# Half of the projections of queries, keys and values moved by one score step in the TensorE order

## The chip, the cores and the metric

The kernel runs on one core of a Trainium2 chip. The metric is the device time of one launch in microseconds (us). Engines are named as in the profile: PE is TensorE (its weight loads are PEld), DVE is VectorE, ACT is ScalarE, POOL is GpSimd, SP is SyncE, which issues the DMAs here.

## The reference

One layer of a macaron block on x of 32 samples, 512 positions, 256 features, in float32: a half-weighted routed feed-forward, attention, and the same feed-forward again, each on the layernorm of its input and added to it.

```python
x = x + 0.5 * ffn(layernorm(x))    # per sample: top 2 of 8 experts, chosen by its first row
x = x + attn(layernorm(x))         # 16 heads of 16, rotary positions, causal softmax
x = x + 0.5 * ffn(layernorm(x))
# attn: q, k, v = split(x @ Wqkv.T); q, k = q * cos + rotate_half(q) * sin, ...
#       out = softmax(mask(q @ k.T / 4)) @ v; return out @ Wo.T
```

## The kernel before, in words

The three parts follow each other; at the two seams they overlap a little. All that is changed lies in the attention.

**Slots.** Attention goes by groups of four heads, four groups to a sample. One turn of the loop is a slot; slot g (0 to 3) of sample s belongs to the group G = 4 s + g. No planner is in play: every engine has its own written order within a slot, and semaphores tie them together. `main` writes the slots of 30 samples out, `lead_in` puts six slots in front, between feed-forward steps. In one slot, three groups are under way:

- group G: the row maxima of its scores. PE computes scores with queries on the partitions (`max_scores`, 11 steps, L1158 to L1167), DVE takes the maximum of each (`maxima`, L996 and L1006).
- group G-2: its scores again, keys on the partitions, with the negative maximum as an added row (`scores`, 10 steps, L1185). ACT takes the exponential of each (`exps`, L1073), POOL masks the diagonal blocks in four pieces (`mask`, L912), and PE multiplies with the values (`probs_v`, L1202). The first of four such products stands in this slot behind step 9, the other three in the next slot.
- group G-3: those three products behind step 3; ACT copies the sum (L1104), PE turns it (`turn_output`, four transposes, L1255) behind step 6, DVE normalises (`normalise_output`, L1016 and L1020). `probs_v` of G-2 writes the same bank and so waits for L1020.

A step is one index n of the loop in PE's `slot`; the text counts from 1, so step 6 is n = 5. `scores` of step n waits for the exponential two steps before (two banks), `max_scores` for the maximum three steps before (three banks).

**Work of other samples in the slots.** The sample that comes next is prepared in the same slots. Slots 0 and 1: its queries and keys, 128 features at a time (`project_qk`, L1219, t = 0 to 3). Each of them is six matmuls 128x512 in two halves of three, one behind an early step and one behind a later step of the slot. Slot 2: its values (`project_v`, L1233), six matmuls 128x256 for each of four blocks of 128 positions. Slot 3: transposes of the sample after that (L1247), and the output projection of the sample before (L1271, L1280). All of these use two banks, `x_ps`.

**Rotary positions.** When both halves of a projection are done (`qk_done`), DVE multiplies by cos (L974) and swaps neighbours (L975) in `begin_rope`, behind maximum 3 or 7 of the slot. POOL (`rope`) multiplies by sin (L920) and adds (L924), between its masks: t = 0 and 2 in the middle of slots 0 and 1, t = 1 and 3 at their end, behind the last mask. ACT rounds to float16 (L1079, `rope_high`), DVE computes what is left over (L981, `rope_low`, behind maximum 1 and 4 of slots 1 and 2). SP writes the result to memory and reads it back into stacks for the next sample's slots.

**Layernorm of the sample after next** stands in slot 2 behind maximum 2: DVE's statistics (L107 to L119), POOL's normalisation (L942, L948).

**Values.** ACT copies the finished values from the bank in `v_copy` (L1122), behind exponentials 5 and 8 of slot 2.

Of the kernel before, what the change touches and what calls it, by code (L numbers as in the profile page):

```python
# [58 lines left out]
def wait(eng, sem, value):  # L59

    if isinstance(value, int) and value <= 0:
        return
    eng.wait_ge(sem, value)
# [690 lines left out]
def attention(nc, ctx, tab, mem, src, dst, cos, sin, first):  # L754
# [49 lines left out]
    def group(G):  # L804
        return not isinstance(G, int) or 0 <= G < B * 4

    def sample(s):
        return not isinstance(s.b, int) or 0 <= s.b < B
# [321 lines left out]
    def tensor(pe):  # L1130
        def part(t, p):
            return t.hi if p == "hi" else t.lo

        def turn_maxima(s, g):

            G = 4 * s.b + g
            pe.wait_ge(max_done, 11 * G)
            nc.tensor.transpose(mx_ps[TURN_BANK][0:NT * GH, 0:P], mx[(g - 1) % 2][:].rearrange("p a i -> p (a i)"),
                                tab.ident[:]).then_inc(mt_done, 1)

        def max_scores(s, g, n):

            G = 4 * s.b + g

            if n == 4:
                wait(pe, mt_copied, G)
            else:
                wait(pe, max_done, 11 * G + (-2, -1, 1, 2, None, 3, 4, 5, 6, 7, 8)[n])
            if n == 0:
                pe.wait_ge(q_stacked, 96 * (s.b + 1))  # L1150
                pe.wait_ge(k_stacked, 96 * (s.b + 1))
            bank = mx_ps[MX_BANK[n]]
            i, heads = (3, [n]) if n < 4 else (2, [n - 4]) if n < 8 else (1, [2 * n - 16, 2 * n - 15]) if n < 10 else (0, range(4))
            w, nh = (i + 1) * P, len(heads)
            half, j = half_of(g)
            rows, const = slice(HP * half, HP * half + TERMS_ROWS), slice(HP * half, HP * half + HP)
            if n < 4:
                nc.tensor.matmul(bank[:, 0:w], q_stack[s.par][rows, j + n % 4, i * P:(i + 1) * P],  # L1158
                                 k_stack[s.par][rows, j + n % 4, 0:w], start=True, stop=True).then_inc(mx_done, 1)
                return  # L1160
            for at, a in enumerate(heads):
                nc.tensor.matmul(bank[:, at * w:at * w + w], q_stack[s.par][rows, j + a, i * P:(i + 1) * P],  # L1162
                                 k_stack[s.par][rows, j + a, 0:w], start=(at == 0), stop=False)

            last = bank[:, 0:nh * w].rearrange("p (a n) -> p a n", a=nh)[:, :, i * P:w]
            over = tab.mask[const, :].rearrange("p (a n) -> p a n", a=1)
            nc.tensor.matmul(last, tab.turn[const, :], over.broadcast_to([HP, nh, P]), start=False, stop=True).then_inc(mx_done, 1)  # L1167

        def scores(s, g, c):

            G = 4 * s.b + g - 2
            ss, sg = of_group(s, g, 2)
            bank = st_ps[c % 2]

            wait(pe, exp_done, 10 * G + c - 1)
            if c == 0:
                pe.wait_ge(rows_set[g % 2], 16 * (2 * s.b + (g - 2) // 2 + 1))
            a = c % 4 if c < 8 else 2 * (c - 8)
            half, j = half_of(sg)
            rows = slice(HP * half, HP * half + TERMS_ROWS + 1)  # L1180

            work = [(a, 0, 0, 0)] if c < 4 else [(a, 1, P, 0), (a, 3, 3 * P, 3 * P)] if c < 8 else \
                [(a, 2, 2 * P, 0), (a + 1, 2, 2 * P, 2 * P)]
            for ha, kt, q0, col in work:
                ins = nc.tensor.matmul(bank[:, col:col + T - q0], k_stack[ss.par][rows, j + ha, kt * P:(kt + 1) * P],  # L1185
                                       q_stack[ss.par][rows, j + ha, q0:T], start=True, stop=True)
            ins.then_inc(st_done, 1)

        def probs_v(s, g, lag, nth, kt):

            G = 4 * s.b + g - lag
            ss, sg = of_group(s, g, lag)
            if kt == 0:

                wait(pe, on_done, G)
                pe.wait_ge(v_copied, 2 * (ss.b + 1))
            pe.wait_ge(exp_done, 10 * G + (4, 8, 10, 8)[kt])
            pe.wait_ge(masked, 4 * G + nth + 1)
            for a in range(GH):
                p = (probs[:, a, :], probs[:, 4 + a, 0:3 * P], probs[:, 8 + a // 2, (a % 2) * 2 * P:(a % 2) * 2 * P + 2 * P],  # L1200
                     probs[:, 4 + a, 3 * P:])[kt]
                ins = nc.tensor.matmul(pv_ps[32 * a:32 * a + 32, kt * P:T], v[ss.par][:, kt, head_of(sg, a), :], p,  # L1202
                                       start=(kt == 0), stop=(nth == 3), tile_position=(0, 32 * a))
            ins.then_inc(pv_done, 1)

        def project_qk(n, t, half):

            idx = 4 * n.b + t
            if t == 0 and not half:
                pe.wait_ge(xT_lo, NC * (n.b + 1))  # L1210
            if n.b == 0 and not half:
                pe.wait_ge(first.xT_lo, NC * (FIRST_LEAD + 4 + t // 2))
            if t < 2 and not half:

                wait(pe, res_done, 2 * (n.b - 2) - 1 + t)
            if t >= 2 and not half:
                pe.wait_ge(rope_in, idx - 1)
            for i, (wp, xp) in enumerate(TERMS):
                ins = nc.tensor.matmul(x_ps[t % 2][:], part(tab.qkv, wp)[:, int(half), t * P:(t + 1) * P],  # L1219
                                       part(xT, xp)[:, int(half), :], start=(i == 0 and not half), stop=(i == 2 and half))  # L1220
            if half:
                ins.then_inc(qk_done, 1)

        def project_v(n, t):

            if t % 2 == 0:
                pe.wait_ge(rope_in, 4 * (n.b + 1) - 1 + t // 2)
                if n.b == 0:
                    pe.wait_ge(first.xT_lo, NC * B)
            i = 0  # L1230
            for c in range(NC):
                for xp, wp in TERMS:
                    ins = nc.tensor.matmul(x_ps[t // 2][:, (t % 2) * D:(t % 2) * D + D], part(xT, xp)[:, c, t * P:(t + 1) * P],  # L1233
                                           part(tab.qkv, wp)[:, c, 2 * D:3 * D], start=(i == 0), stop=(i == 3 * NC - 1))
                    i += 1
            if t % 2:
                ins.then_inc(v_done, 1)
# [48 lines left out]
        def slot(s, g, between=None):  # L1286
            G = 4 * s.b + g
            cur, run = group(G), group(G - 2)
            if G == 0:
                pe.wait_ge(first.gelu_done, 8 * B)  # L1290
            if G == 2:
                pe.wait_ge(stacks_set, 32)
                pe.wait_ge(first.out_done, 2 * B)
            if G == 6:
                pe.wait_ge(stacks_set, 64)
            before = group(G - 3)
            for n in range(11):
                if between:
                    between(n)
                if run and n < 10:  # L1300
                    scores(s, g, n)
                if cur:
                    max_scores(s, g, n)
                if n == 2 and before:
                    probs_v(s, g, 3, 1, 1)
                if n == 1 and group(G - 1):
                    turn_maxima(s, g)
                if n == 2 and before:
                    probs_v(s, g, 3, 2, 3)
                    probs_v(s, g, 3, 3, 2)  # L1310
                if n == 5 and before:
                    turn_output(s, g)
                if g < 2 and sample(s + 1) and n in (0, 1, 4, 5):
                    project_qk(s + 1, 2 * g + (n > 3), half=(n in (1, 5)))
                if g == 2 and sample(s + 1) and n in (0, 1, 4, 5):
                    project_v(s + 1, (0, 1, 4, 5).index(n))
                if g == 3 and sample(s + 2) and n == 0:
                    transposes(s + 2)
                if run and n == 8:
                    probs_v(s, g, 2, 0, 0)  # L1320
                if g == 3 and sample(s + -1) and n == 4:
                    transpose_o(s + -1, s)
                if g == 3 and sample(s + -1) and n >= 9:
                    project_o(s + -1, 2 * (n - 9))
                    project_o(s + -1, 2 * (n - 9) + 1)
# [285 lines left out]
```

## Time and profile before

| | |
|---|---|
| time, median of 3 runs | 2292.76 us (2287.46 to 2299.47) |
| the profiled execution | 2291.23 us, span 2289.5 us |
| PE busy | 2109.5 us, 92% |
| DVE busy | 1931.8 us, 84% |
| ACT busy | 1354.4 us, 59% |
| POOL busy | 1306.6 us, 57% |
| chain that ended last | PE 45%, DVE 33%, SP queue 7%, issue 6%, DMA 5%, ACT 4% |

Busy times are summed over the span of one profiled execution. Matmuls are pipelined and their ends are modelled, so a busy PE need not be one at its peak. The chain is followed back from the last instruction: at each step to what released it, or to the instruction before it on its engine. The stretch from 560 to 1806 us is attention alone; what lies before and behind is feed-forward and the two seams.

### The profile page before, as it was taken

Reading aid. Unit: us, or ns where it says so; the run is one execution under the profiler, and the core shown is the slowest. Engines: PE = TensorE matmul, PEld = TensorE weight load, DVE = VectorE, ACT = ScalarE, POOL = GpSimd, SP = SyncE. Lnnn points to the kernel's source line nnn. Section 1 sums busy time; section 2 is a strip of 40 time slices with the busy share of each in tenths; the row PEclk is TensorE's granted clock in tenths of the full one; section 3 lists DMA queues with packets and bytes.
Section 4 is the critical chain, followed back from the end, with each engine's and each line's share of the span. In section 5 each row is a group of like instructions: output and inputs, shape, how many; then the busy total and the mean of one; then the engine's idle time right before and its main releaser. Section 6 shows DMA issues by size and latency. Waiting matters only on the chain.

```text
span 2289.5 us, 52899 instructions
## 1 busy us (share of the span) xinstructions
PE 2109.5 (92%) x17682; PEld 1141.4 (50%) x17682; DVE 1931.8 (84%) x4485; ACT 1354.4 (59%) x2568; POOL 1306.6 (57%) x1462
## 2 busy tenths in 40 slices
PE   4999999889999999999999999999999888999999
PEld 2666666434444444444444444444444434666666
DVE  6777788788999899999989998999999865777776
ACT  3455444266667666666666676666666655445553
POOL 6666667454555455456545554554555425666664
PEclk9999999899999999999999999999999999999999
DMA  6656666444445444444444454444445423666665
GB/s 208 192 192 207 201 203 200 116 89 89 98 95 101 94 94 98 89 94 93 99 89 100 95 101 94 96 92 96 93 94 98 99 70 118 197 202 194 204 207 167
DMA packets 280391, 295.29 MB, mean 129 GB/s; under 512 B 45784, under 2 KB 263224, under 8 KB 280120
## 3 DMA queue, kind: packets, MB, share of 16 engines
q1 hardware_dynamic: 280120, 291.90, 50.3%
q8 instruction: 143, 2.34, 0.5%
q14 instruction: 128, 1.05, 0.2%
HBM read 140.08 MB, written 83.89 MB: 98 GB/s over the span
## 4 chain that ended last, share of the span: by engine, by line
PE 45%; DVE 33%; SPq 7%; issue 6%; DMA 5%; ACT 4%; DVEq 0%; ACTq 0%
PE bank L710 8%; DVE bank L996 7%; DVE at_mx L1006 7%; PE bank L728 7%; PE bank L1185 6%; PE bank L1202 6%; PE bank L1219 4%; PE bank L1280 4%; ACT probs L1073 3%; DVE turned L975 3%; DVE v_qk L981 3%; DVE turned L974 2%; DVE at_stats L107 2%; PE bank L1255 2%; PE bank L1167 2%
## 5 line engine op out<-in xcount | busy, mean ns | idle before, releaser
L1073 ACT ACTIVATE probs<-bank 128x512 f32<-128x512 f32 x1280 | 747.0, 603 | 456.9 <-PE bank L1185 447.5
L912 POOL TENSOR_SCALAR_AFFINE_SELECT probs<-probs 128x512 f32<-128x512 f32 x512 | 320.4, 638 | 661.1 <-ACT probs L1073 659.3
L1006 DVE TENSOR_REDUCE at_mx<-bank 128x1 f32<-128x384 f32 (+2 forms) x896 | 509.6, 608 | 78.5 <-PE bank L1167 77.0
L1185 PE MATMUL bank<-stacks 49*128 49x512 f16 (+3 forms) x2048 | 458.7, 302 | 71.4 <-ACT probs L1073 71.0
L996 DVE CUSTOM_DVE_ANT_0 bank<-bank,xn 128x512 f32<-128x512 f32 x512 | 351.6, 698 | 38.8 <-PE bank L1158 36.2
L1185 PEld LDWEIGHTS bank<-stacks 49*128 49x128 f16 x2048 | 136.0, 94 | 458.6 <-ACT probs L1073 334.2
L1162 PE MATMUL bank<-stacks 48*128 48x384 f16 (+2 forms) x1536 | 307.7, 275 | 22.1 <-DVE at_mx L1006 15.6
L1167 PE MATMUL bank<-mask,turn 64*128 64x128 bf16 (+2 forms) x896 | 230.7, 257 | 0.0
L1158 PE MATMUL bank<-stacks 48*128 48x512 f16 x512 | 198.5, 389 | 10.6 <-DVE at_mx L996 6.4
L924 POOL TENSOR_TENSOR turned<-turned 128x512 f32<-128x512 f32 x128 | 184.7, 1443 | 19.1 <-POOL turned L920 0.4
L628 ACT ACTIVATE turned<-bank,b1s 128x512 f32<-128x512 f32 x128 | 88.2, 689 | 181.0 <-PE bank L710 179.3
L920 POOL TENSOR_TENSOR turned<-turned,at_sin 128x512 f32<-128x512 f32 x128 | 178.8, 1397 | 27.7 <-DVE turned L975 27.7
L628 ACT ACTIVATE probs<-bank,b1s 128x512 f32<-128x512 f32 x128 | 88.1, 688 | 178.9 <-PE bank L710 177.3
L710 PE MATMUL bank<-stacks 128*128 128x512 f16 x768 | 172.9, 382 | 19.3 <-DVE stacks L568 15.5
L728 PE MATMUL bank<-stacks,v_qk 128*128 128x256 f16 x1536 | 172.7, 273 | 0.0
L1202 PE MATMUL bank<-probs,v_qk 128*32 128x512 f32 (+3 forms) x2048 | 168.6, 448 | 0.0
L1202 PE MATMUL bank<-probs,v 128*32 128x512 f32 (+3 forms) x2048 | 164.3, 439 | 0.0
L728 PEld LDWEIGHTS bank<-stacks,v_qk 128*128 128x128 f16 x1536 | 150.3, 98 | 17.3
L1162 PEld LDWEIGHTS bank<-stacks 48*128 48x128 f16 x1536 | 110.7, 94 | 52.5 <-DVE at_mx L1006 27.0
L710 PEld LDWEIGHTS bank<-stacks 128*128 128x128 f16 x768 | 73.9, 98 | 108.9 <-DVE stacks L568 19.1
L483 POOL TENSOR_TENSOR f_rstd<-f_ve,minus_half 128x4 f32<-128x4 f32 x64 | 91.1, 1424 | 59.4 <-DVE f_ve L119 59.4
L710 PE MATMUL bank<-xThi,w1hi 128*128 128x512 f16 x256 | 99.1, 387 | 25.2 <-DVE xTlo L568 10.6
(145 smaller groups left out, 4619.6 us busy)
## 6 DMA issues: line engine op xcount, KB each, us to landing
stacks<-qk_image SPq DMA_DIRECT2D x384, 128.0 KB, 4.5
qk_image<-v_qk SPq DMA_DIRECT2D x128, 256.0 KB, 3.7
stacks<-w_hi SPq DMA_DIRECT2D x192, 128.0 KB, 3.7
stacks<-w_lo SPq DMA_DIRECT2D x192, 128.0 KB, 3.8
b2s<-in_b SPq DMA_DIRECT2D x128, 128.0 KB, 3.9
after_ffn<-probs SPq DMA_DIRECT2D x32, 512.0 KB, 6.5
at_x<-after_ffn SPq DMA_DIRECT2D x32, 512.0 KB, 4.1
late_x<-after_ffn SPq DMA_DIRECT2D x32, 512.0 KB, 4.7
```

What stands on the lines that cost most here:

```text
L710: ins = nc.tensor.matmul(h_ps[j][:], w, v, start=(n == 0), stop=(n == 3 * NC - 1))
L728: ins = nc.tensor.matmul(y_ps[t // 2][:, t % 2, :], v, w, start=(n == 0), stop=(n == 11))
L912: nc.gpsimd.affine_select(out=ap, in_=ap, compare_op=ALU.is_ge, fill=0.0, base=0, pattern=[[0, d] for d in dims] + [[1, P]], channel_multi ...
L924: nc.gpsimd.tensor_tensor(rotated[t % 2][:], by_cos[t % 2][:], by_sin[t % 2][:], ALU.add).then_inc(rope_done, 1)
L996: nc.vector.tensor_tensor_reduce(out=bank[:, 0:w], in0=bank[:, 0:w], in1=over[:, T - w:T], scale=1.0, scalar=LOWEST, op0=ALU.add, op1=ALU. ...
L1006: nc.vector.tensor_reduce(o_ap, i_ap, AX_X, ALU.max).then_inc(max_done, 1)
L1073: nc.scalar.activation(probs[:, c, :], st_ps[c % 2][:], ACT.Exp, scale=DH ** -0.5).then_inc(exp_done, 1)
L1158: nc.tensor.matmul(bank[:, 0:w], q_stack[s.par][rows, j + n % 4, i * P:(i + 1) * P], k_stack[s.par][rows, j + n % 4, 0:w], start=True, sto ...
L1162: nc.tensor.matmul(bank[:, at * w:at * w + w], q_stack[s.par][rows, j + a, i * P:(i + 1) * P], k_stack[s.par][rows, j + a, 0:w], start=(at ...
L1167: nc.tensor.matmul(last, tab.turn[const, :], over.broadcast_to([HP, nh, P]), start=False, stop=True).then_inc(mx_done, 1)
L1185: ins = nc.tensor.matmul(bank[:, col:col + T - q0], k_stack[ss.par][rows, j + ha, kt * P:(kt + 1) * P], q_stack[ss.par][rows, j + ha, q0:T ...
L1202: ins = nc.tensor.matmul(pv_ps[32 * a:32 * a + 32, kt * P:T], v[ss.par][:, kt, head_of(sg, a), :], p, start=(kt == 0), stop=(nth == 3), ti ...
```

## The change

In PE's `slot` the four calls for the next sample stood behind steps 1, 2, 5 and 6. They now stand behind steps 1, 2, 5 and 7. So in slots 0 and 1 the second half of t = 1 and t = 3, and in slot 2 the last block of values, move from behind step 6, where they followed `turn_output`, to behind the scores and maxima matmuls of step 7. The order on the other engines, all waits and all DMAs stay as they are.

```diff
-                if g < 2 and sample(s + 1) and n in (0, 1, 4, 5):
-                    project_qk(s + 1, 2 * g + (n > 3), half=(n in (1, 5)))
-                if g == 2 and sample(s + 1) and n in (0, 1, 4, 5):
-                    project_v(s + 1, (0, 1, 4, 5).index(n))
+                if g < 2 and sample(s + 1) and n in (0, 1, 4, 6):
+                    project_qk(s + 1, 2 * g + (n > 3), half=(n in (1, 6)))
+                if g == 2 and sample(s + 1) and n in (0, 1, 4, 6):
+                    project_v(s + 1, (0, 1, 4, 6).index(n))
```

## Rows read from the trace of the kernel before

**Rows 1.** Busy us of each engine (instructions) in one period, granted clock, DMA share, GB/s

```profile
1005.00:1050.03 45.03, 42.09 (x394) 19.57 (x392) 41.40 (x102) 30.15 (x61) 24.34 (x29) 1.00 0.45 93
```

**Rows 2.** Timeline of PE: start, us, engine, line, operation, count [idle before <-releaser]

```profile
599.91 1.09 PE L1247 MATMUL bank<-ident,at_xn 128*128 128x128 f32 x8
...
1770.90 1.09 PE L1247 MATMUL bank<-ident,at_xn 128*128 128x128 f32 x8
```

**Rows 3.** Chain of waits in a period: start, us, what was on the chain

```profile
1009.18 0.14 issue
...
1023.51 0.59 PE bank L1255 x4
1024.10 0.65 PE bank L1219 x3
...
1045.94 0.66 PE bank L1233 x6
```

**Rows 4.** Timeline of PE in slot 0, steps 6, 7 and 9

```profile
1023.44 0.66 PE L1255 MATMUL bank<-ident,at_o 128*128 128x128 f32 x4
...
1024.68 0.33 PE L1185 MATMUL bank<-stacks 49*128 49x384 f16 x1
...
1025.82 0.28 PE L1185 MATMUL bank<-stacks 49*128 49x256 f16 x1 [0.52 <-ACT probs L1073]
```

**Rows 5.** Timeline of DVE, slot 0 and the head of slot 1

```profile
1024.50 0.42 DVE L1020 TENSOR_TENSOR on<-bank,at_inverse 128x256 f32<-128x256 f32 x1
1025.15 0.56 DVE L1006 TENSOR_REDUCE at_mx<-bank 128x1 f32<-128x384 f32 x1 [0.22 <-PE bank L1167]
...
1029.73 1.19 DVE L981 TENSOR_TENSOR v_qk<-turned,v_qk 128x512 f16<-128x512 f32 x1
```

**Rows 6.** Timeline of POOL: sample 0, then slots 0 to 2 of a later sample

```profile
457.74 0.64 POOL L912 TENSOR_SCALAR_AFFINE_SELECT probs<-probs 128x512 f32<-128x512 f32 x1 [5.08 <-ACT probs L1073]
...
1028.50 0.64 POOL L912 TENSOR_SCALAR_AFFINE_SELECT probs<-probs 128x512 f32<-128x512 f32 x1 [0.85 <-ACT probs L1073]
1029.10 1.27 POOL L920 TENSOR_TENSOR turned<-turned,at_sin 128x512 f32<-128x512 f32 x1
...
1033.98 1.78 POOL L920 TENSOR_TENSOR turned<-turned,at_sin 128x512 f32<-128x512 f32 x1
...
1038.81 0.64 POOL L912 TENSOR_SCALAR_AFFINE_SELECT probs<-probs 128x512 f32<-128x512 f32 x1 [0.45 <-ACT probs L1073]
...
1040.83 1.73 POOL L924 TENSOR_TENSOR turned<-turned 128x512 f32<-128x512 f32 x1
...
1044.34 0.64 POOL L912 TENSOR_SCALAR_AFFINE_SELECT probs<-probs 128x512 f32<-128x512 f32 x1 [1.78 <-ACT probs L1073]
```

**Rows 7.** Timeline of PE in slot 1 (first two) and slot 2

```profile
1033.75 0.66 PE L1255 MATMUL bank<-ident,at_o 128*128 128x128 f32 x4
...
1036.56 1.06 PE L1202 MATMUL bank<-probs,v_qk 128*32 128x512 f32 x8
...
1048.11 1.06 PE L1202 MATMUL bank<-probs,v 128*32 128x512 f32 x8
```

**Rows 8.** Timeline of DVE: sample 0, then slots 1 and 2 of a later sample

```profile
457.75 0.64 DVE L119 SCALAR_TENSOR_TENSOR at_ve<-at_pair 128x4 f32<-128x4 f32 x1
...
1033.95 0.68 DVE L981 TENSOR_TENSOR v_qk<-turned,v_qk 128x512 f16<-128x512 f32 x1
...
1035.83 0.42 DVE L1020 TENSOR_TENSOR on<-bank,at_inverse 128x256 f32<-128x256 f32 x1
...
1040.73 0.69 DVE L981 TENSOR_TENSOR v_qk<-turned,v_qk 128x512 f16<-128x512 f32 x1
...
1043.38 0.17 DVE L111 TENSOR_TENSOR at_pair<-at_stats 128x4 f32<-128x4 f32 x1
...
1044.08 0.16 DVE L119 SCALAR_TENSOR_TENSOR at_ve<-at_pair 128x4 f32<-128x4 f32 x1
...
1047.30 0.42 DVE L1020 TENSOR_TENSOR on<-bank,at_inverse 128x256 f32<-128x256 f32 x1
```

## The prediction

> **What bounds the kernel now.** I read first the busy time by stretch, for one sample of the attention, because all that is moved lies there. In one period of 45.03 us TensorE is busy 42.09 and VectorE 41.40 [rows 1]: neither leaves more than 4 us, and the granted clock is 1.00, so the order in which they hand work to each other sets the time, and a move can matter. The period is steady: the first transposes of two samples 26 periods apart lie 1170.99 us apart, 45.04 each [rows 2].
>
> Then the chain of waits over one sample. In slot 0 it runs on TensorE through the output's transposes (0.59) and the moved half projection (0.65), then on VectorE through all of slot 1; in slot 2 it comes back to TensorE, again through transposes and projection (0.66) [rows 3]. In slots 0 and 2 the moved work is on the chain, in slot 1 it is not. Last I read the timelines of the engines in a period, to see what stands behind each hand-over.
>
> **What the change does.** It adds and removes no instruction, wait or DMA. In three of four slots, TensorE issues three matmuls 128x512 (or six 128x256) behind score step 7 instead of step 6; they pass the scores and maxima matmuls of step 7 alone, and no other queue is passed. Two consumers wait: VectorE's begin_rope behind its maximum 7, and ScalarE's second v_copy behind exponential 8. Queued behind begin_rope are maxima 8 to 11, which the maxima matmuls of step 11 and of step 1 of the next slot wait for; behind v_copy, exponential 9.
>
> **Slot 0.** Transposes begin at 1023.44 and take 0.59 [rows 3, 4], so scores of step 7 can start at 1024.03 instead of 1024.68: 0.65 earlier. VectorE waited 0.22 for them before maximum 7 and has nothing else in the way, so it gains 0.22 [rows 5]. Step 9 waited 0.52 for the exponential of step 7 [rows 4]. That exponential now starts 0.65 earlier, and TensorE has the projection to do meanwhile: the same matmuls without the wait, step 9 at about 1025.3 instead of 1025.82. I take **0.5** gained on TensorE from step 9 on (0.52 at most), and with it on exponential 10, on the mask behind it and on GpSimd's rope multiply at 1029.10, since GpSimd sat 0.85 idle before that mask [rows 6]. begin_rope comes behind a maximum of 0.56, so not before 1025.4; the projection is through at about 1025.2, before step 9. Should it be late, the next paragraph has room for it.
>
> At the head of slot 1 VectorE's rope_low (L981) took 1.19 where the one of slot 2 took 0.69: it started at 1029.73 inside GpSimd's multiply (1029.10 to 1030.37) and ended 0.55 behind its end [rows 5, 6, 8]. With VectorE 0.22 and GpSimd 0.5 earlier it still starts inside, so its end follows GpSimd: **-0.5 us**, even if VectorE gained nothing. Were there no such tie, it would be -0.22, the other end.
>
> **Slot 1.** From there VectorE runs without a gap, so all on it is 0.5 earlier; I go on in its time, as if nothing had moved. TensorE went from the transposes at 1033.75 to probs_v of the group at 1036.56 in 2.81, of which 0.52 were the wait that goes: 2.29, so 1036.04, and up to 0.3 later, because at the slot's head it waits for maxima that gained only 0.22. But the bank of probs_v is free only when VectorE's L1020 is done, at 1035.83 + 0.42 = 1036.25. From 0 to 0.14 behind that (0.14 is the longest hand-over from VectorE to TensorE on the chain) is 1036.25 to 1036.39: 0.17 to 0.31 earlier than before [rows 3, 7, 8]. Nothing on the chain waits for this in slot 1. But one thing follows it at a fixed distance: probs_v, scores 10, exponential 10, mask, rope multiply, rope add (L924). The add started at 1040.83, 4.27 behind probs_v, and GpSimd was idle for 0.45 before the mask, so it can come earlier by all of it: at 1040.52 to 1040.66 [rows 6, 7].
>
> VectorE's rope_low of slot 2 started at 1040.73 [rows 8]. Before, it was 0.10 ahead of the add and ran in 0.69, and the add took 1.73. Now the add is 0.07 to 0.21 ahead. Whether 0.07 decides, the trace can say: at 457.74 a GpSimd mask led a VectorE operation by 0.01 and that one took 0.64 instead of 0.16 [rows 6, 8]; the loser is blocked for the whole of the winner. So rope_low ends at 1040.59 + 1.27 + 0.55 = 1042.41 instead of 1041.42: **+1.0 us**, on the chain.
>
> The Trainium skill states this as a rule (SBUF — State Buffer, section "SBUF: two separate sides"): VectorE operations with two SBUF inputs and GpSimd operations that read SBUF take one port pair as a lock, and whichever starts first holds it for its whole instruction. This trace agrees (1.19 against 0.69, 0.64 against 0.16), and it is the rule that speaks against this change: without the lock slot 2 would lose nothing.
>
> **Slot 2.** VectorE is 1.0 late there against its own time. The small layernorm operations, L111 at 1043.38 before, then come at 1044.4, just behind the mask that GpSimd runs from 1044.34 to 1044.98 (fixed by TensorE's scores 4, which do not move); L111 too has two SBUF inputs [rows 6, 8]. It would end with the mask: 1044.98 instead of 1044.55 (1043.55 + 1.0): **+0.4 us**; 0 if it slips in first. I take 0.4, as the row at 457.74 is the nearest. Step 6 of TensorE waits for the maximum behind them. Behind it the projection (0.66) leaves the chain, but probs_v then waits for L1020, whose end is 1047.30 + 0.42 = 1047.72: it starts at 1047.8 against 1048.11, **-0.3 us** and not -0.66 [rows 7, 8]. If the hand-over is 0.14, -0.25. v_copy still comes behind exponential 8: nothing. Slot 3 is untouched and passes on what slot 2 hands it.
>
> **Sum.** -0.5 + 1.0 + 0.4 - 0.3 = +0.6 us per sample. Of the 31 samples that are projected after the lead-in I count 29 (in the first two the phases differ), 29 x 0.6 = +17.4 us. The profiled execution has 2291.23 us around a span of 2289.5; the median of three is 2292.76. On the median this is 2310 us. Its own range: without the 0.4 it is +0.2 per sample, 2299; without slot 2's gain +0.9, 2319.
>
> **Rivals.**
> - *The lock goes the old way* (faster). If the hand-over to probs_v takes over 0.21, or the add's 0.07 does not count, rope_low keeps its 0.69 and slot 2 its small operations: -0.5 - 0.3 = -0.8 per sample, 31 x 0.8 = -25 us: **2268**. For it: at the second rope_low of slot 1 VectorE led by 0.03, 1033.95 against 1033.98, and won [rows 6, 8], so the deciding distance is not known to better than some hundredths. Against it: every step of the 4.27 us is a wait that the trace shows without slack. It decides at one point, the order of two starts at the head of slot 2.
> - *Gains and losses cancel* (same). The lock bites by 1.0, the small operations escape and the slot 2 gain is whole (0.5 rather than 0.3): 0.0 per sample, **2293**.
> - *The change does nothing on the chain* (same): if maximum 6 rather than 7 held VectorE, slot 0 would gain nothing. The 0.22 before maximum 7 with TensorE as its end speaks against it [rows 5]; the rest would be as in one of the others.
>
> **How the numbers follow.** Chances: forecast 0.60, the lock the old way 0.30, cancelling 0.07, nothing 0.03. Half a per cent (11 us) is what a measurement of this kernel tells from no change. Of the forecast's share 0.10 falls short of it (only the lock's 1.0, +6 us). So faster 0.30, same 0.10 + 0.07 + 0.03 = 0.20, slower 0.50. The likeliest case alone ranges from 2299 to 2319; the stated range has to hold the first rival as well and goes from 2266 to 2320.
>
> **What would show it.** In the timelines of a period: step 9 of slots 0 to 2 no longer waits for an exponential; the first rope_low of slot 1 still takes over 0.9; GpSimd's add at the head of slot 2 starts before rope_low and takes 1.27, rope_low some 1.7; transposes of successive samples 45.6 apart. If that rope_low takes 0.69 and the period is 44.2, the order of two starts was read wrongly and the first rival holds. If maximum 7 of slot 0 still waits for TensorE, the first step is wrong.

## The result, and the profile after

The changed kernel takes **2339.23 us** (median of 4 runs, 2333.81 to 2348.97) against 2290.49 us for the kernel before in the same session. The ratio is 1.0211 (95% interval 1.0165 to 1.0257): slower, by some 2%. The forecast was slower, 2310 us, with a range up to 2320; the time lies 19 us above the range. The profiled execution takes 2337.15 us around a span of 2335.4 us.

The page first: the head, the busy times, the granted clock in 40 slices, and the chain by engine.

```profile
span 2335.4 us, 52899 instructions
...
PE 2157.0 (92%) x17682; PEld 1145.8 (49%) x17682; DVE 1967.4 (84%) x4485; ACT 1357.4 (58%) x2568; POOL 1304.8 (56%) x1462
...
PEclk9999999899999999999999999999999979999999
...
PE 45%; DVE 36%; issue 6%; SPq 6%; DMA 4%; ACT 3%; DVEq 0%; ACTq 0%
```

TensorE's busy time rose by 47.5 us, although it has the same matmuls to do. So its matmuls took longer, and the slices of the clock line do not tell why, for each averages over 58 us. VectorE's busy time rose by 35.6 us: operations of it are blocked inside. Two stretches of one period each, with the columns of [rows 1], show both.

```profile
971.42:1017.11 45.69, 42.47 (x393) 19.40 (x393) 42.61 (x102) 30.25 (x61) 24.26 (x29) 1.00 0.47 94
1017.11:1064.11 47.00, 43.87 (x394) 19.85 (x393) 42.81 (x102) 30.26 (x61) 24.28 (x29) 0.96 0.44 91
```

The kernel now has **two lengths of period**. The first, 45.69 us at a clock of 1.00, is the one that was forecast (45.6), and VectorE is 1.2 us busier in it than before. In it TensorE is 0.38 us busier than before at the same clock, so a part of the 47.5 us (some 11 us in 29 samples) is not the clock's. The second has VectorE within 0.2 us of the first but TensorE another 1.40 us busier, at a mean clock of 0.96. Of 25 periods from 600.52 to 1766.26, 16 take 47.0 to 47.1 us, 7 take 45.7 to 45.9, one 44.23 and one 48.61; their mean is 46.63, against 45.04 before [rows 2]. That is +1.59 us, and 29 samples of it are 46 us.

The steps of the forecast, row by row: TensorE at steps 8 and 9 of slot 0; then VectorE's maximum 7 there, its first `rope_low` in slot 1, and its `rope_low` and L111 in slot 2.

```profile
991.36 0.33 PE L1185 MATMUL bank<-stacks 49*128 49x384 f16 x1
...
991.59 0.27 PE L1185 MATMUL bank<-stacks 49*128 49x256 f16 x1
```

```profile
991.09 0.55 DVE L1006 TENSOR_REDUCE at_mx<-bank 128x1 f32<-128x384 f32 x1
...
995.65 1.03 DVE L981 TENSOR_TENSOR v_qk<-turned,v_qk 128x512 f16<-128x512 f32 x1
...
1006.51 1.66 DVE L981 TENSOR_TENSOR v_qk<-turned,v_qk 128x512 f16<-128x512 f32 x1
...
1010.14 0.64 DVE L111 TENSOR_TENSOR at_pair<-at_stats 128x4 f32<-128x4 f32 x1
```

Step 9 has no bracket (no wait) any more, where [rows 4] had 0.52 of waiting; maximum 7 has none, where [rows 5] had 0.22; the first `rope_low` takes 1.03, so the tie to GpSimd's multiply is still there. The last two VectorE rows are the head of slot 2: `rope_low` takes 1.66 instead of 0.69 and L111 0.64 instead of 0.17 [rows 8]. Beside them stand these rows of GpSimd: the last mask of slot 1, the rope multiply and add, and the first mask of slot 2.

```profile
1004.35 0.63 POOL L912 TENSOR_SCALAR_AFFINE_SELECT probs<-probs 128x512 f32<-128x512 f32 x1 [0.20 <-ACT probs L1073]
1004.95 1.27 POOL L920 TENSOR_TENSOR turned<-turned,at_sin 128x512 f32<-128x512 f32 x1
1006.37 1.26 POOL L924 TENSOR_TENSOR turned<-turned 128x512 f32<-128x512 f32 x1
1010.12 0.63 POOL L912 TENSOR_SCALAR_AFFINE_SELECT probs<-probs 128x512 f32<-128x512 f32 x1 [2.50 <-ACT probs L1073]
```

The add starts at 1006.37, `rope_low` at 1006.51: GpSimd leads by 0.14, inside the forecast 0.07 to 0.21, keeps its 1.26 and blocks VectorE (the lock of the prediction: the later of the two starts waits). The mask leads L111 by 0.02 and blocks that one too. All this was forecast, and it is so in every sample but one of the stretch from 560 us on: GpSimd leads by 0.13 to 0.15, and `rope_low` takes 1.66 to 1.68. In the one at 869.5 VectorE leads:

```profile
869.50 0.69 DVE L981 TENSOR_TENSOR v_qk<-turned,v_qk 128x512 f16<-128x512 f32 x1
...
869.65 1.68 POOL L924 TENSOR_TENSOR turned<-turned 128x512 f32<-128x512 f32 x1 [0.44 <-POOL turned L920]
```

There the add comes 0.44 behind the multiply instead of some 0.15 (before, that sample's add is late by the same 0.29). `rope_low` keeps 0.69, TensorE waits 0.18 at step 6, and this is the period of 44.23 us: the kernel itself shows what the order is worth.

What was not forecast stands on TensorE, at the maxima matmul of step 6 of slot 2, which waits for the maximum behind those two operations. Here it is in two successive samples.

```profile
1012.19 0.33 PE L1162 MATMUL bank<-stacks 48*128 48x384 f16 x1 [1.60 <-DVE at_mx L996]
...
1013.55 0.27 PE L1233 MATMUL bank<-qkv_hi,at_xTlo 128*128 128x256 f16 x1
...
1057.89 0.33 PE L1162 MATMUL bank<-stacks 48*128 48x384 f16 x1 [1.60 <-DVE at_mx L996]
...
1059.61 0.42 PE L1233 MATMUL bank<-qkv_hi,at_xTlo 128*128 128x256 f16 x1
```

TensorE stands still for 1.60 us in both. In the first the same matmul of the values takes 0.27 afterwards, in the second 0.42. The windows behind the wait show why (columns as in [rows 1]; the granted clock is the third number from the end).

```profile
1012.00:1016.00 4.00, 3.72 (x33) 1.68 (x33) 3.90 (x12) 1.92 (x5) 3.72 (x6) 1.00 1.03 146
...
1058.00:1062.00 4.00, 4.00 (x26) 1.84 (x24) 3.51 (x9) 1.08 (x2) 2.85 (x5) 0.58 1.14 157
...
1060.00:1062.00 2.00, 2.00 (x15) 0.85 (x12) 1.51 (x4) 0.66 (x2) 1.06 (x2) 0.50 1.10 189
```

In the second sample the granted clock is 0.50 between 1060 and 1062: the lower of the two levels, 1.2 GHz instead of 2.4. TensorE gets 26 matmuls through in 4 us instead of 33. Over the attention, TensorE waits at this place for 40.2 us in 26 turns where it was 4.9 in 27, after and, in the second fence, before (the columns are us in total, times, longest us):

```profile
PE bank L1162 <- DVE at_mx L996: 40.2, 26, 1.6
...
PE bank L1185 <- ACT probs L1073: 15.7, 27, 0.6
```

```profile
PE bank L1185 <- ACT probs L1073: 58.2, 109, 0.6
...
PE bank L1162 <- DVE at_mx L996: 4.9, 27, 0.2
```

The wait of L1185 for an exponential is the one that the move takes away, 42 us of it. But waiting removed is only a gain where it lies on the chain.

### The profile page after: what moved, and what is told of

Read it like the earlier page. It is cut to its first block, busy times and chain, and to the rows that moved or that the text cites. A ratio compares the mean times of both kernels' runs of the same rounds, so it can differ in the third digit from the quotient of the medians.

```text
span 2335.4 us, 52899 instructions
## 1 busy us (share of the span) xinstructions
PE 2157.0 (92%) x17682; PEld 1145.8 (49%) x17682; DVE 1967.4 (84%) x4485; ACT 1357.4 (58%) x2568; POOL 1304.8 (56%) x1462
## 4 chain that ended last, share of the span: by engine, by line
PE 45%; DVE 36%; issue 6%; SPq 6%; DMA 4%; ACT 3%; DVEq 0%; ACTq 0%
PE bank L710 9%; DVE at_mx L1006 8%; PE bank L728 7%; DVE bank L996 7%; PE bank L1185 6%; PE bank L1202 6%; DVE v_qk L981 4%; PE bank L1280 4%; PE bank L1219 3%; DVE turned L975 3%; DVE turned L974 2%; ACT probs L1073 2%; DVE at_stats L107 2%; PE bank L1167 1%; PE bank L1247 1%
## 5 line engine op out<-in xcount | busy, mean ns | idle before, releaser
L1185 PE MATMUL bank<-stacks 49*128 49x512 f16 (+3 forms) x2048 | 469.5, 309 | 24.2 <-ACT probs L1073 23.9
L1162 PE MATMUL bank<-stacks 48*128 48x384 f16 (+2 forms) x1536 | 318.9, 283 | 68.7 <-DVE at_mx L996 47.2
L1185 PEld LDWEIGHTS bank<-stacks 49*128 49x128 f16 x2048 | 138.8, 95 | 415.2 <-ACT probs L1073 309.5
L1167 PE MATMUL bank<-mask,turn 64*128 64x128 bf16 (+2 forms) x896 | 236.9, 264 | 0.0
L924 POOL TENSOR_TENSOR turned<-turned 128x512 f32<-128x512 f32 x128 | 171.9, 1343 | 19.1 <-POOL turned L920 0.4
L1202 PE MATMUL bank<-probs,v_qk 128*32 128x512 f32 (+3 forms) x2048 | 174.5, 461 | 1.6
L1202 PE MATMUL bank<-probs,v 128*32 128x512 f32 (+3 forms) x2048 | 169.3, 449 | 1.6
L981 DVE TENSOR_TENSOR v_qk<-turned,v_qk 128x512 f16<-128x512 f32 x128 | 128.5, 1004 | 1.0 <-ACT v_qk L1079 1.0
```

Source lines behind the costliest of these rows:

```text
L981: nc.vector.tensor_tensor(qk.lo[:, t, :], rotated[t % 2][:], qk.hi[:, t, :], ALU.subtract).then_inc(qk_lo, 1)
```

## The experiments

Two theories were set against each other. **Lock and clock**: the move gains in slots 0 and 2; in slot 1 it brings GpSimd's add ahead of `rope_low`, VectorE loses some 1.4 us in slot 2, TensorE stands still for it, and on top of that its clock falls. **The move itself**: the moved projections behind step 7 cost TensorE time directly, in each slot alike, or the clock falls because work was taken from behind step 6. Ratios are to the kernel before in the same session.

### The move in slots 0 and 2 alone

```diff
+                late = 6 if g == 0 else 5
-                if g < 2 and sample(s + 1) and n in (0, 1, 4, 5):
-                    project_qk(s + 1, 2 * g + (n > 3), half=(n in (1, 5)))
+                if g < 2 and sample(s + 1) and n in (0, 1, 4, late):
+                    project_qk(s + 1, 2 * g + (n > 3), half=(n in (1, late)))
-                if g == 2 and sample(s + 1) and n in (0, 1, 4, 5):
-                    project_v(s + 1, (0, 1, 4, 5).index(n))
+                if g == 2 and sample(s + 1) and n in (0, 1, 4, 6):
+                    project_v(s + 1, (0, 1, 4, 6).index(n))
```

> The kernel before, with the half projection moved behind step 7 in slots 0 and 2 alone; slot 1 keeps it behind step 6. Theory (lock and clock): the loss comes from slot 1's move alone, which lets GpSimd's rope add start ahead of VectorE's rope_low at the head of slot 2. Without it rope_low keeps 0.69 us, the small layernorm operations are not blocked, TensorE's wait before maximum 6 of slot 2 stays near 0.2 us and the granted clock at 1.00; the gains of slots 0 and 2 stay: 0.5 + 0.3 per sample, period 44.2 us, time about 2266. Rival (the place behind step 7 itself costs, in each slot alike): two thirds of the 47 us remain, about 2322. Rival (the clock falls by itself with the load): faster periods but the granted clock still near 0.97 and samples 1.4 us apart, about 2290.

Measured: **2264.02 us** (2261.69 to 2266.28), ratio 0.9875 (0.9836 to 0.9914). This is faster than both kernels, by 1.25% against the kernel before. VectorE and GpSimd at the head of slot 2, and TensorE at step 6:

```profile
1023.25 0.69 DVE L981 TENSOR_TENSOR v_qk<-turned,v_qk 128x512 f16<-128x512 f32 x1
...
1025.90 0.17 DVE L111 TENSOR_TENSOR at_pair<-at_stats 128x4 f32<-128x4 f32 x1
```

```profile
1023.42 1.65 POOL L924 TENSOR_TENSOR turned<-turned 128x512 f32<-128x512 f32 x1
```

```profile
1027.48 0.33 PE L1162 MATMUL bank<-stacks 48*128 48x384 f16 x1 [0.18 <-DVE at_mx L996]
```

`rope_low` leads by 0.17 and runs in 0.69; the add is the one that is stretched. TensorE waits 0.18, the clock is 1.00 over the whole attention, and the period is 44.25: -0.79 us, the forecast's -0.5 - 0.3. So the move as such costs nothing in two of its three slots.

### The move in slot 1 alone

```diff
+                late = 6 if g == 1 else 5
-                if g < 2 and sample(s + 1) and n in (0, 1, 4, 5):
-                    project_qk(s + 1, 2 * g + (n > 3), half=(n in (1, 5)))
+                if g < 2 and sample(s + 1) and n in (0, 1, 4, late):
+                    project_qk(s + 1, 2 * g + (n > 3), half=(n in (1, late)))
```

> The kernel before, with the half projection moved in slot 1 alone. Theory (lock and clock): the order of the two starts flips as in the full change, slot 2 loses 1.0 + 0.4 us to the lock and the clock falls in some two of three samples at 1.36 us each, with none of the gains of slots 0 and 2: about +2.3 us per sample, some 2360, slower than the full change. Rival (the place behind step 7 costs in each slot alike): a third of the 47 us, about 2306.

Measured: **2367.97 us** (2362.93 to 2384.12), ratio 1.032 (1.0278 to 1.0363). GpSimd, VectorE, and the whole attention:

```profile
1025.98 1.27 POOL L924 TENSOR_TENSOR turned<-turned 128x512 f32<-128x512 f32 x1
```

```profile
1026.12 1.67 DVE L981 TENSOR_TENSOR v_qk<-turned,v_qk 128x512 f16<-128x512 f32 x1
...
1029.76 0.62 DVE L111 TENSOR_TENSOR at_pair<-at_stats 128x4 f32<-128x4 f32 x1
```

```profile
560.00:1780.00 1220.00, 1117.00 (x9959) 514.38 (x9959) 1088.15 (x2559) 761.54 (x1522) 613.35 (x731) 0.96 0.43 89
```

All of the loss, and none of the gain, comes with slot 1: GpSimd leads by 0.14, and the clock falls to a mean of 0.96. Where it does not fall the period is 46.46 us, +1.43 for the lock alone (45.02 once, in the sample in which VectorE leads); where it falls, 47.8 to 50.2 us. So a fall costs more here than the 1.36 us of the full change, up to 3.7 us, and the time is 8 us above the 2360 that was expected; the profiled execution is the slowest of the four (2384.12 us). The two halves add up: -26.9 and +77.1 us make +50.2; the full change cost +48.7. That they meet so closely is partly chance: the four times of this kernel lie 21 us apart.

### The full change, with GpSimd's add made to wait for `rope_low`

```diff
-            wait(pool, qk_lo, idx - 1)
+            wait(pool, qk_lo, idx if t == 3 and n.b else idx - 1)
             pool.wait_ge(sin_done, idx + 1)
             nc.gpsimd.tensor_tensor(rotated[t % 2][:], ...).then_inc(rope_done, 1)
```

> The changed kernel whole, and GpSimd's last rope add of a sample (t = 3) also waits until VectorE's rope_low of t = 2 is done, so VectorE goes first at the head of slot 2. Theory (lock and clock): all of the loss goes and the gains stay: period 44.2 us, about 2266, clock 1.00. Rival (place behind step 7 costs): no better than the changed kernel, 2337 or more. Rival (the lock alone, the clock falls for another reason): the 1.4 us of the lock go, the 1.36 us of the clock stay in two of three samples, about 2293.

Measured: **2268.91 us** (2262.48 to 2274.62), ratio 0.9899 (0.9854 to 0.9944). VectorE, then GpSimd:

```profile
1029.74 0.68 DVE L981 TENSOR_TENSOR v_qk<-turned,v_qk 128x512 f16<-128x512 f32 x1
...
1032.39 0.17 DVE L111 TENSOR_TENSOR at_pair<-at_stats 128x4 f32<-128x4 f32 x1
```

```profile
1030.51 1.28 POOL L924 TENSOR_TENSOR turned<-turned 128x512 f32<-128x512 f32 x1 [1.06 <-DVE v_qk L981]
```

Every projection is moved here, slot 1's too, and GpSimd waits 1.06 us in this place; the time is that of the move in slots 0 and 2 (the intervals overlap). With VectorE first, the blocked operations, the stand-still and the fall of the clock are all gone (clock 1.00, period 44.24). The order of these two starts is what the whole loss hangs on.

### The full change, with TensorE kept busy during the stand-still

```diff
+                if g == 2 and n == 5 and sample(s + 1) and s.b >= 0:
+                    for i in range(12):
+                        nc.tensor.matmul(x_ps[1][:, D:2 * D], xT.hi[:, 0, 0:P],
+                                         tab.qkv.hi[:, 0, 2 * D:3 * D], start=True, stop=True)
                 if cur:
                     max_scores(s, g, n)
```

The results of the twelve matmuls are not used. The lock stays as the change has it; only the clock should differ.

> The changed kernel, with 12 matmuls 128x256 (1.3 us, results unused, overwritten by the projection) on TensorE in slot 2 ahead of the maxima matmul of step 6, where it stands idle for 1.60 us. They shorten no wait and add work. Theory (the clock falls because TensorE stands idle there): the granted clock stays at 1.00, all samples 45.7 us apart, about 2311, that is the loss of the lock alone. Rival (the clock falls by itself with load or time): the clock still falls in two of three samples, 2337 or more.

Measured: **2309.74 us** (2305.3 to 2312.58), ratio 1.0079 (1.0051 to 1.0107). VectorE, blocked as before, TensorE, and the whole attention:

```profile
1002.17 1.67 DVE L981 TENSOR_TENSOR v_qk<-turned,v_qk 128x512 f16<-128x512 f32 x1
...
1005.80 0.63 DVE L111 TENSOR_TENSOR at_pair<-at_stats 128x4 f32<-128x4 f32 x1
```

```profile
1006.18 1.48 PE L1304 MATMUL bank<-qkv_hi,at_xThi 128*128 128x256 f16 x12
...
1007.85 0.33 PE L1162 MATMUL bank<-stacks 48*128 48x384 f16 x1 [0.18 <-DVE at_mx L996]
```

```profile
560.00:1780.00 1220.00, 1171.87 (x10780) 546.48 (x10778) 1136.03 (x2693) 807.05 (x1600) 648.97 (x774) 1.00 0.45 94
```

TensorE waits 0.18 where it waited 1.60, the clock stays at 1.00, and 25 of 27 periods take 45.67 to 45.69 us (one takes 45.25, the sample in which VectorE leads, one 45.91): **+0.65 us**, the forecast's +0.6. Work that nobody needs makes the changed kernel 29 us faster. The difference to the full change is the clock's share; what is left, 19 us, is the lock less the gains of slots 0 and 2. The same matmuls in another place were not tried; that the gap itself matters and not the added work is shown by this experiment together with the one before it, where the gap is gone and nothing is added.

### The kernel before, with the lock's effect made by a wait

```diff
         dve.wait_ge(qk_hi, 4 * n.b + t + 1)
+        if t == 2 and n.b:
+            dve.wait_ge(rope_done, 4 * n.b + 4)
```

No matmul is moved. `rope_low` of slot 2 waits until GpSimd's add is done. Lines are two higher here.

> The kernel before with nothing moved: only VectorE's rope_low of t = 2 (head of slot 2) also waits until GpSimd's add of t = 3 is done, so that GpSimd goes first there by a plain wait. Theory (lock and clock): rope_low ends some 1.4 us later than before, L111 then comes while the mask runs, TensorE stands idle about 1.6 us before maximum 6 of slot 2, and the granted clock falls there in part of the samples, though no matmul was moved: +1.45 us per sample for the order and some 0.9 for the clock, about 2363; without the clock 2336. Rival (the fall of the clock needs the moved projections, e.g. their place after the wait): 2336 and the clock at 1.00 in slot 2.

Measured: **2359.24 us** (2358.66 to 2374.65), ratio 1.032 (1.029 to 1.035). VectorE and GpSimd at the head of slot 2 of one sample, TensorE at its step 6, and the windows behind that step and behind the same step of another sample:

```profile
640.55 0.69 DVE L983 TENSOR_TENSOR v_qk<-turned,v_qk 128x512 f16<-128x512 f32 x1 [1.32 <-issue]
...
643.21 0.17 DVE L111 TENSOR_TENSOR at_pair<-at_stats 128x4 f32<-128x4 f32 x1
```

```profile
642.70 0.64 POOL L912 TENSOR_SCALAR_AFFINE_SELECT probs<-probs 128x512 f32<-128x512 f32 x1 [2.24 <-ACT probs L1075]
```

```profile
644.79 0.33 PE L1164 MATMUL bank<-stacks 48*128 48x384 f16 x1 [1.14 <-DVE at_mx L998]
```

```profile
645.00:649.00 4.00, 3.69 (x24) 2.18 (x23) 3.35 (x9) 0.88 (x2) 2.76 (x5) 0.57 1.10 183
1167.00:1171.00 4.00, 3.48 (x36) 1.79 (x36) 3.84 (x10) 2.13 (x5) 3.66 (x7) 1.00 1.12 182
```

A part of the expectation missed: L111 takes its 0.17 (it comes 0.51 behind the mask's start and not 0.02, with 0.13 of the mask left); TensorE stands still for 1.14 and not 1.60. The clock falls all the same, in many samples (0.57 in the first window) and not in others (1.00 in the second, behind a wait of 1.13). Without the clock's share the time was put at 2336. The periods say the same: 46.5 us where the clock stays, +1.45 for the order alone, and 47.6 to 48.0 where it falls. So the clock falls because TensorE waits for VectorE in slot 2, and not because a projection was taken from behind step 6: here it is still there.

### Slot 0 alone, slot 2 alone

The edits are the two halves of the first experiment.

> The kernel before, with the half projection moved in slot 0 alone. Theory: this is the term of 0.5 us per sample: GpSimd's rope multiply starts 0.5 earlier and with it the blocked rope_low at the head of slot 1 ends 0.5 earlier; period 44.5, about 2275. Other end: VectorE's own 0.22 alone, period 44.8, 2284. The order at the head of slot 2 stays VectorE first.

> The kernel before, with the last block of values moved in slot 2 alone. Theory: this is the term of 0.3 us per sample, since probs_v then waits for L1020 instead of the exponential: period 44.73, about 2282. Rival (the whole 0.5 us wait goes): period 44.5, 2275. Rival (nothing): 45.0, 2291.

Measured: slot 0 **2278.98 us** (2271.72 to 2293.06), ratio 0.9952 (0.9935 to 0.9969), period 44.57; slot 2 **2280.44 us** (2278.74 to 2285.91), ratio 0.9954 (0.9939 to 0.9968), period 44.71. Against 45.03 that is -0.46 and -0.32, together -0.78, the -0.79 of the two at once. In time, slot 0 lies between the two ends that were put for it; the period decides: its gain is 0.46 and not the 0.22 by which VectorE waited. It comes through the tie to GpSimd's multiply, which `rope_low` outlasts by 0.55 as before:

```profile
1019.28 1.27 POOL L920 TENSOR_TENSOR turned<-turned,at_sin 128x512 f32<-128x512 f32 x1
...
1020.07 1.03 DVE L981 TENSOR_TENSOR v_qk<-turned,v_qk 128x512 f16<-128x512 f32 x1
```

With slot 2 alone, `probs_v` waits for L1020 there, as the forecast has it: it starts 0.06 behind its end.

```profile
1043.35 0.42 DVE L1020 TENSOR_TENSOR on<-bank,at_inverse 128x256 f32<-128x256 f32 x1
...
1043.83 1.07 PE L1202 MATMUL bank<-probs,v 128*32 128x512 f32 x8
```

## Why the prediction was right in its steps and wrong in the time

- **Slot 0, -0.5:** measured alone -0.46. Right, mechanism and size. (VectorE's own gain before that is not 0.22 but 0.31: maximum 7 starts 1.40 behind the transposes, 989.69 in the changed kernel, instead of 1.71. The tie hides it.)
- **Slot 1, GpSimd's add 0.07 to 0.21 ahead:** it is 0.14 ahead. The path is the one that was summed up: L1020 ends at 1002.04, `probs_v` starts at 1002.10, the add 4.27 behind it. Right; that slot 1 alone brings it about is shown by moving slot 1 alone, and by its absence when the other two are moved.
- **`rope_low` +1.0 and L111 +0.4:** 1.66 - 0.69 = +0.97 and 0.64 - 0.17 = +0.47. Right.
- **Slot 2, -0.3 and not -0.66:** measured alone -0.32. Right.
- **Sum +0.6 per sample, 2310 us:** with the clock held at 1.00 it is +0.65 and 2309.74 us.
- **The step that failed** is the premise of the first paragraph, "the granted clock is 1.00", carried through the sum as if it could not change, and with it in slot 2 "Step 6 of TensorE waits for the maximum behind them", priced at the length of the wait alone. The lengthened wait is in the sum, and rightly; the clock behind it was put at nothing without a reason. The wait grew from 0.18 to 1.60 us, and behind it the granted clock fell to 0.50 in most samples: in the window of 4.00 us at a mean of 0.58 for (1.00 - 0.58) / 0.50 x 4.00 = 3.4 us. In the 16 periods of 47.0 to 47.1 us this costs 47.05 - 45.69 = 1.36 us; over all 25 the mean is 46.63 - 45.69 = **+0.94 us per sample**, the missing term. With it the sum is +1.59, and 29 of them on 2291.23 are 2337 us, as the profiled execution has it (2337.15).

The trace of before could have warned. From 560 us on the waits at step 6 were all 0.2 or less, but not in `lead_in`. There stands the very row from which the prediction took the lock, the blocked operation at 457.75 [rows 8]. Step 6 of TensorE waits behind it, and then the clock falls:

```profile
459.11 0.41 PE L1162 MATMUL bank<-stacks 48*128 48x384 f16 x1 [1.02 <-DVE at_mx L996]
```

```profile
456.00:458.00 2.00, 1.59 (x14) 0.73 (x12) 1.90 (x11) 2.00 (x5) 0.26 (x1) 1.00 0.55 127
...
460.00:462.00 2.00, 2.00 (x13) 0.82 (x11) 1.54 (x4) 0.40 (x1) 2.00 (x4) 0.50 1.15 133
```

The clock is 1.00 before that wait of 1.02 us and 0.50 from 460 to 466, in a stretch less dense than the steady one. So an estimate was to be had: 6 us at half the rate lose 3 us, so between nothing and some 3 us per sample.

On the lock, the first rival differed by the sign of a lead of some hundredths; the runs put the truth on the forecast's side. The rule of the Trainium skill (SBUF — State Buffer, "SBUF: two separate sides") is borne out again: when VectorE starts first, by 0.17, the add takes 1.65 instead of 1.27; when GpSimd starts first, by 0.14, `rope_low` takes 1.66 instead of 0.69.

**Open:** why the clock falls in some samples and not in others behind the same wait of 1.60 us (and in the experiment with the added wait behind 1.13 to 1.14). The waits of the two samples above do not tell them apart before the fall. The falls are not scattered: in the changed kernel they come mostly in pairs with one undisturbed sample between, in the experiment with the added wait in two unbroken rows of eight and more. What sets that order no run tested. Open too is why the add of the sample at 869.5 comes late, before and after.

The Trainium skill (TensorE: Matmul & The Clock Gate, Part 1) says that the gate answers to how busy TensorE has lately been and that the same kernel can meet it in different phases from run to run. The first half agrees with the twelve matmuls that kept the clock at 1.00; no run here shows the second.

## What to carry to other kernels

Where a change lengthens a wait of TensorE in an otherwise dense stretch, price the wait twice: its length, and what the matmuls behind it cost at the lower clock level; and look at the clock in short windows behind the wait, since forty slices of a whole span average it away. Where VectorE and GpSimd work on SBUF side by side, look at which of two operations starts first and by how much: an earlier engine that is off the chain can take the lock from one that is on it, and a wait added to the former (here 1.06 us on GpSimd) is then a gain. Test a move slot by slot: here slots 0 and 2 were worth 1.25%, and slot 1 alone cost more than twice that.

## What the runs showed that was not expected

- The granted clock fell from 1.00 to 0.50 behind a stand-still of TensorE of 1.60 us, in another kernel of 1.14 us, and in a stretch of the kernel before of 1.02 us. Behind 1.60 and 1.14 us it fell in about two of three samples, and filling the gap with twelve unused matmuls (1.48 us) kept it at 1.00 in all.
- A fall of the clock has no fixed price: 1.36 us per sample in the full change, up to 3.7 us where slot 1 alone was moved.
- The order of two starts decided without an exception: in the seven kernels where `rope_low` and the add of slot 2 overlap, from 560 us on, the one that began first kept its time and the other was stretched, at leads down to 0.09 us.
